# Redrawn instruction orders for a two-layer attention and expert kernel, with the closing flag read earlier

## What is computed

```python
def gat_layer(x, adj, W, a_self, a_neigh, b):
    feat = jnp.einsum('nf,hfo->hno', x, W)
    e = jax.nn.leaky_relu(attn_self[:, :, None] + attn_neigh[:, None, :], 0.2)
    e = e + MASK_VAL * (1.0 - adj)[None, :, :]          # MASK_VAL = -1e10
    out = jnp.einsum('hnm,hmo->hno', softmax(e), feat) + b[:, None, :]
    return jax.nn.elu(concat_heads(out))
x = x + vmap(two gat layers)(ctx_512, layernorm(x))
gate, up = split(einsum('bgeh,ehd->bged', layernorm(x), gate_up_proj))
x = x + einsum('bgei,eih->bgeh', silu(gate) * up, down_proj)
```

## Time and profile before

| | |
|---|---|
| device time, three runs | 220.61, 221.28, 222.46 us; median 221.28 us |
| device time of the profiled execution | 221.49 us |
| its span | 219.7 us, so 1.79 us lie outside it |
| PE busy | 204.8 us (93% of the span), 890 matmuls |
| DVE, ACT, POOL busy | 153.9, 103.4, 102.7 us |
| last matmul of `last_down` ends | 213.97 us after the start of the span |

### The profile page before, as it was taken

How to read it: one execution, slowest core, us unless ns; L and a number is a source line. 1 busy time by engine, 2 the same in 40 slices (tenths; PEclk the granted TensorE clock), 3 DMA queues, 4 the chain that set the end, 5 groups by cost and what they waited for, 6 DMA issues and landing times.

```text
span 219.7 us, 2706 instructions
## 1 busy us (share of the span) xinstructions
PE 204.8 (93%) x890; PEld 159.2 (72%) x890; DVE 153.9 (70%) x286; ACT 103.4 (47%) x159; POOL 102.7 (47%) x82
## 2 busy tenths in 40 slices
PE   7897899979979899999999999999999999999990
PEld 2345677856658677888888888888888888888860
DVE  0678999867999845899968947999788861510140
ACT  3799999989738332114164044653254031112100
POOL 2000968398967768898059310588035412202200
PEclk9999999999999999999999999999999999999998
DMA  6999889663622858779997365652892300140014
GB/s 203 328 428 400 230 261 349 242 107 84 125 67 64 201 128 222 111 148 160 220 373 288 107 236 162 240 224 95 296 355 117 95 2 0 55 139 0 0 69 132
DMA packets 15203, 38.80 MB, mean 177 GB/s; under 512 B 2768, under 2 KB 2768, under 8 KB 14160
## 3 DMA queue, kind: packets, MB, share of 16 engines
q1 hardware_dynamic: 12080, 34.10, 44.1%
q0 software_dynamic: 2816, 4.20, 13.6%
q10 hardware_dynamic: 288, 0.26, 0.4%
HBM read 30.16 MB, written 8.40 MB: 176 GB/s over the span
## 4 chain that ended last, share of the span: by engine, by line
PE 62%; DVE 17%; POOL 6%; ACT 5%; issue 4%; DMA 3%; SPq 0%; POOLq 0%; DVEq 0%
PE bank L1695 30%; PE bank L1709 15%; PE bank L1656 6%; PE bank L1682 5%; DVE hexp L1227 4%; DVE found L1256 4%; DVE val L1246 3%; DVE top L1252 3%; PE bank L1645 3%; DMA f_table<-f_row 2%; POOL ff_row L808 2%; ACT hexp L933 2%; PE bank L1739 2%; POOL x_sb L820 1%; DVE f_row L1260 1%
## 5 line engine op out<-in xcount | busy, mean ns | idle before, releaser
L1695 PE MATMUL bank<-acts,ring 128*128 128x512 f32 x288 | 67.2, 390 | 0.0
L1695 PEld LDWEIGHTS bank<-acts,ring 128*128 128x128 f32 x288 | 53.9, 188 | 11.2
L1631 PE MATMUL bank<-wide,acts 128*128 128x512 f32 x192 | 48.9, 405 | 5.3 <-ACT bank L959 2.0
L1631 PEld LDWEIGHTS bank<-wide,acts 128*128 128x128 f32 x192 | 35.4, 188 | 18.1 <-issue 5.2
L795 POOL TENSOR_TENSOR ring<-ring_raw,ring 128x1024 fp32r<-128x1024 f32 x13 | 32.6, 2518 | 31.7 <-ACT ring L926 31.7
L1709 PE MATMUL bank<-ring,wide 128*128 128x512 f32 x144 | 34.7, 392 | 0.0
L926 ACT CAST ring<-ring_raw 128x1024 fp32r<-128x1024 f32 x24 | 24.7, 1059 | 18.0 <-DMA ring_raw<-in_down_t 11.9
L1709 PEld LDWEIGHTS bank<-ring,wide 128*128 128x128 f32 x144 | 26.7, 188 | 5.4
L820 POOL DMA_INDIRECT x_sb<-y_table,ff_row x16 | 25.1, 1569 | 5.0 <-issue 4.2
L1656 PE MATMUL bank<-ring,first_xnT 128*128 128x512 f32 x96 | 23.4, 396 | 1.0 <-DVE first_xnT L1286 1.0
L1306 DVE TENSOR_TENSOR hexp<-bank,hexp 128x512 f32<-128x512 f32 x12 | 8.2, 684 | 21.0 <-PE bank L1695 21.0
(11 more groups left out here) (86 smaller groups left out, 246.3 us busy)
## 6 DMA issues: line engine op xcount, KB each, us to landing
ring_raw<-in_gate_up_t SPq DMA_DIRECT2D x16, 512.0 KB, 6.1
x_sb<-in_x SPq DMA_DIRECT2D x4, 1024.0 KB, 9.7
ring_raw<-in_down_t SPq DMA_DIRECT2D x8, 512.0 KB, 6.0
y_table<-val SPq DMA_DIRECT2D x16, 256.0 KB, 3.5
out<-x_sb SPq DMA_DIRECT2D x16, 256.0 KB, 2.8
val<-in_x SPq DMA_DIRECT2D x4, 1024.0 KB
ctxT<-in_ctx_t SPq DMA_DIRECT2D x4, 256.0 KB, 5.8
wide_raw<-in_W_t SPq DMA_DIRECT2D x2, 512.0 KB, 7.6
```

The lines of the kernel that those rows point to most:

```text
L1631: last = nc.tensor.matmul(bank[Y_BANK[n]][:, :], hT[:, b % 2, c, w, t * P:(t + 1) * P], W1p[:, c, v, :], start=False, stop=(c == KC - 1 an ...
L1695: last = nc.tensor.matmul(bank[(UP_BANK if half else GATE_BANK)[KC * e + c]][:, :], ring[:, r % RING, w, col:col + P], xnT[:, (e - 1) % 2, ...
```

## The change

All edits lie in orders, in bank numbers, in the split of the low parts, and in the place of the flag. No arithmetic, tile or DMA is added or taken away, but for one wait on PE at the very end.

1. **Split of the low parts.** `h_low` of the first batch's chunks 1 and 3, and of 9 and 10, go to POOL, those of 11 and 12 to DVE (DVE has six instead of eight). `r_low` stays 11 on DVE, but of the first nine (those of expert 0 and the first of expert 1) DVE has 1, 2, 3, 7 in place of 1, 3, 5, 6, 7, 8. `inner_low`: DVE has 6, 7, 11 to 14 instead of 4 to 11.
2. **Order of the loads.** `load_r(6)` and the bias go ahead of `load_ctx(1)`, `load_x(3)` and more ring tiles ahead of the first store, `load_x(1)` behind `load_x(3)`; `store_y(0)` behind `store_f(0)`; `load_ctx(3)` right behind `store_f(0)`.
3. **Order on PE.** `layer1_part(0, 0)` comes ahead of `layer0(1, 0)`, `layer0(3, 0)` ahead of `layer1(5)`; `first_gate(0)` no longer splits layer 2 but comes after `layer1(15)`; `turn_inner(2)`, `first_down(2)` move ahead of `gate(1, 0)`.
4. **Orders on DVE, ACT, POOL** follow this: all `find_top`, `find_row` and `rows(3)` come before `y_value(12)` and before the ring's low parts; every `y_exp_of` comes before `first_silu(0)`; POOL has `r_low(6)` and `r_low(8)` between gathers.
5. **The end.** `count_sure` moves from before the last `last_down` to behind `down_of(3, 0)`. SP and DVE read the flag and branch before their last four stores and outputs, which are put on both branches. PE waits for all stores after its branch.

```diff
-        R_LO_DVE = (1, 3, 5, 6, 7, 8, 11, 15, 19, 20, 23)
-        H_LO_DVE = (0, 1, 2, 3, 9, 10, 14, 15)
-        IN_LO_DVE = (4, 5, 6, 7, 8, 9, 10, 11)
+        R_LO_DVE = (1, 2, 3, 7, 13, 15, 16, 18, 19, 20, 22)
+        H_LO_DVE = (0, 2, 11, 12, 14, 15)
+        IN_LO_DVE = (6, 7, 11, 12, 13, 14)
...
-        def unless_sure(engine, program):
+        def unless_sure(engine, program, last=None):
             engine.wait_ge(flag_made, 1)
             n_sure = engine.value_load(flag[0:1, 0:1])
             with engine.If(n_sure < B * N):
+                if last:
+                    last()
                 engine.wait_ge(out_stored, 16 * B * E)
                 program(engine)
+            if last:
+                with engine.Else():
+                    last()
...
 (POOL)
+            h_low(0, 1)
+            h_low(0, 3)
             h_low(1, 0)
-            r_low(0)
             h_low(1, 1)
...
 (ACT, after h_exp_of(0, 1))
+            seed(0)
+            h_high(0, 0)
             h_exp_of(0, 2)
...
 (ACT)
             h_exp_of(1, 3)
+            h_high(1, 0)
             h_below(1, 2)
             h_below(1, 3)
+            act.wait_ge(h_made, 6)
+            seed(1)
             y_exp_of(0)
...
 (PE)
             layer0(0, 3)
+            layer1_part(0, 0)
+            pe.wait_ge(h_made, 1)
             layer0(1, 0)
...
-            layer1_part(12, 0)
-            layer1_part(12, 1)
-            first_gate(0)
-            layer1_part(12, 2)
-            layer1_part(12, 3)
             layer1(13)
             layer1(14)
             layer1(15)
+            pe.wait_ge(y_made, 14)
+            turn_xn(0, 1)
             pe.wait_ge(xnT_lo, 1)
-            turn_xn(0, 1)
+            first_gate(0)
             first_up(0)
...
             down_of(3, 0)
-            up(3, 3)
+            pe.wait_ge(in_made, 15)
+            count_sure()
             down_of(3, 1)
...
             last_down(3, 3)
             unless_sure(pe, general.tensor)
+            pe.wait_ge(out_stored, 16 * B * E)
```

More of the change, by code:

```diff
@@ L874, in _ @@
-            follow(2, 2)
-            gather(2, 1)
-            follow(2, 3)
-            gather(0, 2)
-            follow(3, 0)
-            follow(3, 1)
-            x2_inverse(0, 2)
-            follow(3, 2)
-            gather(3, 0)
-            gather(3, 1)
-            follow(3, 3)
+            h_low(2, 1)
+            h_low(2, 2)
+            follow(1, 0)
+            gather(0, 0)
+            gather(0, 1)
+            follow(1, 1)
+            r_low(4)
+            r_low(5)
+            gather(1, 1)
@@ new lines, in _ @@
+            x2_inverse(0, 0)
+            follow(2, 0)
+            h_low(3, 1)
+            follow(2, 1)
+            gather(1, 0)
+            r_low(6)
+            r_low(8)
+            gather(2, 0)
+            x2_inverse(0, 1)
+            follow(3, 0)
+            gather(2, 1)
+            follow(1, 2)
+            follow(1, 3)
+            x2_inverse(0, 2)
+            gather(3, 0)
+            follow(2, 2)
+            follow(3, 1)
+            follow(3, 2)
+            follow(0, 2)
+            follow(0, 3)
@@ L1124, in _ @@
             seed(13)
+            y_exp_of(12)
+            turned_xn(0, 0)
+            act.wait_ge(y_made, 13)
             seed(14)
-            first_silu(0)
-            y_exp_of(12)
+            seed(15)
             y_exp_of(13)
-            act.wait_ge(y_made, 14)
-            seed(15)
             y_exp_of(14)
@@ L1426, in _ @@
+            y_value(3)
+            rows(1)
             h_value(2, 1)
             h_value(2, 2)
+            find_top(2, 0)
+            find_top(2, 1)
+            find_row(2, 0)
+            find_row(2, 1)
             y_value(4)
-            find_row(1, 3)
-            r_low(1)
             h_value(2, 3)
-            y_value(5)
-            h_low(2, 1)
-            h_low(2, 2)
-            rows(1)
-            y_value(6)
-            r_low(3)
-            find_top(2, 0)
-            y_value(7)
@@ L1469, in _ @@
-            normalize(0, 1)
+            y_value(8)
+            h_value(3, 1)
+            h_value(3, 2)
+            x2_moments(0, 0)
             find_row(3, 2)
             find_top(3, 3)
-            r_low(5)
+            y_value(9)
+            h_value(3, 3)
+            normalize(0, 0)
+            h_low(3, 0)
+            h_low(3, 2)
+            h_low(3, 3)
+            y_value(10)
+            find_row(3, 3)
+            y_value(11)
+            rows(3)
+            r_low(1)
             y_value(12)
-            find_row(3, 3)
+            turned_low(0, 0)
@@ L1475, in _ @@
+            r_low(2)
+            x2_stats(0, 1)
             y_value(13)
-            rows(3)
-            r_low(6)
-            x2_stats(0, 2)
+            x2_moments(0, 1)
+            r_low(3)
             y_value(14)
-            x2_moments(0, 2)
+            normalize(0, 1)
             r_low(7)
             y_value(15)
+            x2_stats(0, 2)
             turned_low(0, 1)
-            r_low(8)
+            x2_moments(0, 2)
             normalize(0, 2)
             first_inner(0)
+            first_inner_low(0)
@@ L1562, in _ @@
             normalize(3, 2)
+            turned_low(2, 2)
+            inner(1, 2)
             normalize(3, 3)
+            r_low(13)
+            turned_low(2, 3)
+            inner_low(1, 2)
             r_low(15)
-            output(1, 0)
-            turned_low(3, 2)
-            turned_low(3, 3)
-            output(1, 1)
+            r_low(16)
             x_stats(1, 0)
@@ L1814, in _ @@
+            pe.wait_ge(xnT_lo, 4)
+            turn_inner(1)
+            pe.wait_ge(in_made, 3)
+            turn_inner(2)
+            turn_xn(1, 0)
+            first_gate(3)
+            pe.wait_ge(out_made, 1)
+            turn_xn(1, 1)
+            first_up(3)
+            pe.wait_ge(xnT_lo, 5)
+            turn_xn(1, 2)
+            turn_xn(1, 3)
             first_down(1)
-            pe.wait_ge(in_made, 3)
-            turn_xn(1, 0)
+            pe.wait_ge(in_made, 4)
+            first_down(2)
@@ L1843, in _ @@
+            pe.wait_ge(out_made, 4)
+            pe.wait_ge(first_in_lo, 4)
+            down_of(1, 0)
+            pe.wait_ge(xnT_lo, 11)
             gate(1, 3)
-            pe.wait_ge(first_in_lo, 3)
-            turn_inner(3)
+            down_of(1, 1)
+            pe.wait_ge(in_made, 7)
+            turn_xn(3, 0)
+            pe.wait_ge(xnT_lo, 12)
             up(1, 3)
-            first_down(3)
+            turn_xn(3, 1)
+            down_of(1, 2)
             pe.wait_ge(in_made, 8)
-            turn_xn(2, 2)
```

579 lines of the change are left out of this document (265 added, 314 removed).

## The result

| | before | predicted | after |
|---|---|---|---|
| median of the runs, us | 221.47 | 216.4 (the forecast alone: 213.9 to 218.6) | 228.06 (six runs, 225.32 to 230.41) |
| profiled execution, us | 221.49 | 216.6 | 227.04 |
| its span, us | 219.7 | | 225.2 |
| mean granted clock of PE | 0.997 | | 0.972 |

A forecast was written before the change was run, and what follows sets the result against it. PE bounds the kernel, with ACT pacing layer 2's first half and DVE its second. 221.49 - 1.2 - 3.1 - 1.0 - 0.6 + 1.0 = 216.6, so 216.4 as median; range 213.9 to 218.6, chance 0.64.

The forecast's parts named there:

- Part 4: The first expert, up to gate(1, 0) at 103.3: 1.0 us gained, 5.4 us gained so far by then.
- Part 1: Start to 18.2 us: nothing gained; bounds 0.5 us lost if ctx(1) is late, 0.5 gained.
- Part 2: First half of layer 2, 18.2 to 52.7 us: 1.2 us gained, layer1(9) ending at 51.5.
- Parts 3 and 4: Layer 2's end, 3.1 us gained with layer1(15) ending at 68.9, and the first expert, 1.0 us gained.
- Part 5: The ring's experts: nothing gained, thin cover, 0 to 0.5 us lost; tightest is the chain for gate(1, 2).
- Part 6: Charge for POOL's extra work up to 66 us holding DVE operations: 1.0 us lost, bounds 0 and 2.2.
- Part 7: The kernel's end, flag load and branch moved under the last matmuls: 0.6 us gained, bounds 0 and 1.0.
- Held by POOL, and slower: Rival: four r_low on DVE before the first gate each held 2.2 us, 8.8 in all: 224.3 us, chance 0.10.
- POOL late: Rival: POOL's full list from 40 to 66 us delivers 4 late, PE idles 3: 219.4 us, chance 0.18.

The follow-up runs named there:

- e15: Kernel after with r_low(6), r_low(8) back on DVE, rows(2) earlier, POOL's inverses ahead of r_low(10), start mended twice: 218.87 us, ratio 0.989.
- e7: Kernel after with layer0(1, 0) ahead of layer1_part(0, 0) on PE, h_high(0, 0) and two exponentials ahead of seed(0) on ACT: ratio 1.0391.
- e14: Kernel before with r_low(6) and r_low(8) moved from DVE to POOL, back to back behind gather(2, 0): 228.11 us, ratio 1.031.
- e9: Kernel after with 28 filler matmuls on PE in front of layer1(14), behind a wait for y_value(9): ratio 1.0397.
- e4: Kernel before with only the change's end (flag and branches earlier, PE waiting for the stores): ratio 0.9991.
- e2: Kernel after with POOL's r_low(6) and r_low(8) moved behind x2_inverse(0, 2): 224.50 us profiled, 227.84 to 232.8 in three more.
- e8: Kernel after with the start reordered, r_low(6) and r_low(8) apart, and POOL's three inverses ahead of r_low(10): 222.74 us, ratio 1.0029.
- e12: Kernel before with r_low(6) and r_low(8) moved from DVE to POOL, behind gather(3, 0): 224.88 us profiled, ratio 1.028.
- e6: Kernel after with POOL's three inverses first, then r_low(10), two inner_low, r_low(11) and r_low(12): 222.83 us, ratio 1.0096.

## Why the prediction was wrong

Milestones of PE, in us; e15 has the change's orders behind 18 us, but for `rows(2)`, `r_low(6)` and `r_low(8)` and POOL's order at 116 us, so that the two long holds are gone. The 208.6 is the last matmul of the kernel before, 213.97, less the 5.4 of Part 4:

| | predicted | after | e15 |
|---|---|---|---|
| `layer1_part(0, 2)` starts | 18.1 | 19.11 | 16.73 |
| `layer1(9)` ends | 51.5 | 51.9 | 51.5 |
| `layer1(15)` ends | 68.9 | 75.1 | 69.5 |
| `gate(1, 0)` starts | 103.3 | 109.65 | 104.97 |
| last matmul ends | 208.6 | 219.5 | 210.5 |

**Part 1 (start, nothing): too good by 1.0.** I had `ctx(1)` landing "by about 10" and the bias early. In the kernel after ACT waited 0.94 us for the bias, `h_low(0, 0)` came at 11.5, and PE stood idle for 3.33 us, longer than the other gaps of its start; in e7 ctx(1) was the last to come, at 10.5. My bound of 0.5 was exceeded.

**Part 2 (1.2 gained): right.** `layer1(9)` ended at 51.9 in spite of the late start. No stall for POOL's `acts` near 45.

**Parts 3 and 4 (3.1 and 1.0 gained): right in the order, wrong in the kernel.** Without the long holds the stages end within 1.7 us of the layout (e15, 69.5 and 104.97). With them, `layer1(15)` came 6.2 us late: 3.18 idle, 1.64 of slow matmuls, 0.4 carried in, and 1.0 of small waits and of a pitch that I took too short (e15 needs 18.0 from `layer1(9)` on, where I had 17.4). I had laid out DVE's list between 59 and 64 with `rows(3)` at 0.15 us and `seed(14)` at 61.9 against a need at 63.3. A cover of 1.4 us stood against one hold of 4.4.

**Part 5 (the ring, 0 to 0.5 lost): wrong by 4.1.** I had named this chain as the tightest, `turned_low(2, 0)` at 116 to 118 against a need at 117.6; it came at 126.62. I had followed who waits in POOL's queue, and not that `r_low(10)`, the inverse and `r_low(11)` and `(12)` run there from 116.43 to 124.93 without a gap, beside two `normalize`. It cost 2.50 us idle and 1.60 of slow matmuls.

**Part 6 (the charge for POOL, 1.0, bounds 0 and 2.2): the step that failed.** The mechanism was named, with the rows that show it; its size and its number were not. I took a hold to be one `r_low` long (3.42 less 1.20 = 2.2, from the earlier trace rows) and allowed at most one. Beyond the instruction's own time the holds were 4.4 us (`rows(3)`), 6.33 less 1.20 = 5.1 (e14) and up to 7.88 less 0.55 = 7.3. Against the 1.0 in the sum, the two holes that they opened in the kernel after cost 3.18 + 1.64 and 2.50 + 1.60, 8.9 us. The row that could have told me was there: `rows(2)`, 3.09 us, ended with *both* of POOL's `h_low`. I read it as a price of an operation, when the hold had gone through two of POOL's instructions. But the other row of the same group shows that a hold need not do so. POOL's three `r_low` from 139.90 run without a gap, and DVE was let in behind each of them, with these two `normalize` and then with the `r_low` of 3.42:

```profile
140.21 4.92 DVE L1278 TENSOR_SCALAR xn<-x_sb,x2mv,rstd 128x512 f32<-128x512 f32 x2
```

So 2.2 was one true size of a hold, and I took it for the only one. What decides whether DVE is let in between two of POOL's instructions stays open. The Trainium skill (SBUF — State Buffer, Who interferes with whom) says that a `tensor_scalar` in its two-port mode and an instruction with two SBUF inputs contend with GpSimd, and the traces agree as to who is held: `rows`, `normalize` and `r_low` were, `y_value` and the statistics of `x2_stats` beside POOL's pairs were not (0.7 us each). No trace shows in which mode a `tensor_scalar` ran. The page lets the holder keep the port for its whole instruction; here DVE sometimes waited through several.

**The clock: missing in the sum.** I priced a stall at its own length. Behind the two later ones of the kernel after, at a granted clock of 0.50, the matmuls took 1.64 and 1.60 us more than at full clock, and e9 shows that this part goes when PE is kept busy. The kernel before has no idle time over 1.46 us behind its start, so nothing in its rows showed it.

**Part 7 (the end, 0.6): 0.2 to 0.3.** Rows of the kernel after, the wait of SP and two branches:

```profile
SPq L641 <- DMA out<-x_sb: 4.1, 1, 4.1
...
L635 DVEq COMPARE_BRANCH  x1: 72/72/72, 211.9 to 211.9; - x1
L635 PEldq COMPARE_BRANCH  x1: 3867/3867/3867, 215.8 to 215.8; - x1
```

SP does not load the flag behind its last store any more, as predicted (a branch of 0.04 us is left there), and DVE's outputs were in time (first at 217.51, straight behind PE). But the wait for the last store is 4.1 us in the kernel after and in e4, and was 3.6 in the kernel before, so that the end behind the last matmul still takes 5.7 in both. Over all traces it takes 5.24 to 5.79 with the new end (fourteen, mean 5.56) and 5.74 to 5.90 with the old (three, mean 5.84), where I had 5.0 to 5.3. Why the landing takes longer stays open.

**The rivals.** "Held by POOL, and slower" (224.3, chance 0.10) is what happened, through `rows` and `normalize`, and in the ring's stage too, not through the four `r_low` I had summed. The argument against it, that DVE was not held from 76 to 105.6 in the kernel before, was sound about that stage and said nothing on the new pairs: POOL had no ring operation there. "POOL late" is what e2, e8 and e12 show, where a gather came late behind an `r_low`.

**The ledger, on the profiled execution.** 216.6 predicted; + 0.4 at 52 us; + 5.8 more at `layer1(15)`; + 0.1 more at `gate(1, 0)`; + 4.6 more at the last matmul, 4.1 of them at 127 us; + 0.6 at the end; - 1.0, the charge already in the sum: 227.1, against 227.04.

## What to carry to other kernels

Before work is given to an engine that shares a port, list for each stretch in which it runs without a gap which instructions of the other engine can be held, and let the bound of the charge be the whole stretch, not one instruction of it (here the other engine was let in after one instruction at some places and after the whole stretch at others); then compare that with the cover of what is queued behind the victim. To open one such stretch was worth 4.2 us here with the same work on the same engines (e6). Charge a stall of PE with its echo at half clock, and test such an order over several runs: which instruction is caught hangs on tenths of a microsecond.
